# Last stage of a four-layer gated kernel: low halves of the expert weights moved to GpSimd, tile flags spread over the first tiles, and a new order of steps

## The reference, cut to what matters

```python
scores = softmax(xf @ gate_w.T)                  # 4096 tokens, 8 experts
top_vals, top_idx = top_k(scores, 2)
w_dense = zeros((T, E)).at[rows, top_idx].set(top_vals)
y, g = split(einsum('td,ehd->teh', xf, W1), 2)   # H = 192
eo = einsum('teh,edh->ted', y * silu(g), W2)
z = einsum('te,ted->td', w_dense, eo)
z = z + gated_mlp(xf, Ws1, Ws2)                  # a shared expert, 384 wide
x = x + tanh(g_ffn[1]) * z
```

## Time and profile before

| | |
|---|---|
| median of 3 runs | 1037.29 us (1036.86 to 1037.44) |
| the profiled execution's own time | 1033.01 us |
| its span | 1031.3 us |
| TensorE matmuls busy | 940.7 us, 91% |
| TensorE weight loads busy | 798.2 us, 77% |
| VectorE busy | 769.5 us, 75% |
| ScalarE busy | 575.9 us, 56% |
| GpSimd busy | 398.8 us, 39% |
| mean granted TensorE clock | 0.963 of full |

### The profile page before, as it was taken

The page is one execution under the profiler, slowest core; times in us unless marked ns, Lnnn a source line. Parts: engine busy times, 40 slices in busy tenths (PEclk is TensorE's granted clock), DMA queues, the critical chain, the costliest instruction groups (busy, mean ns, idle before and its releaser), DMA issues.

```text
span 1031.3 us, 22818 instructions
## 1 busy us (share of the span) xinstructions
PE 940.7 (91%) x6365; PEld 798.2 (77%) x6365; DVE 769.5 (75%) x2336; ACT 575.9 (56%) x1344; POOL 398.8 (39%) x571
## 2 busy tenths in 40 slices
PE   4999999999998756999999999997999995999995
PEld 3666666666665434999999999987888884999995
DVE  3677777777775325788888888889878878888884
ACT  1688888888886632344344344443555632666663
POOL 1011111111111001354445345445577651777775
PEclk9999999999999767999999999999999997999998
DMA  7664754755730250001001001100124445777775
GB/s 216 165 156 119 173 134 122 167 136 126 165 100 1 62 174 27 27 28 53 26 26 53 26 26 41 39 7 2 33 77 134 140 138 191 126 125 129 129 128 68
DMA packets 91811, 98.41 MB, mean 95 GB/s; under 512 B 14992, under 2 KB 85472, under 8 KB 91744
## 3 DMA queue, kind: packets, MB, share of 16 engines
q1 hardware_dynamic: 77504, 79.11, 29.4%
q0 software_dynamic: 13680, 17.84, 10.1%
q10 hardware_dynamic: 560, 0.66, 0.2%
HBM read 30.18 MB, written 59.01 MB: 86 GB/s over the span
## 4 chain that ended last, share of the span: by engine, by line
PE 55%; DVE 5%; issue 1%; ACT 1%; POOL 1%; DMA 1%; POOLq 0%; DVEq 0%; ACTq 0%
PE c_out L1351 3%; PE c_turned L1362 3%; PE c_cross L1351 3%; PE c_mlp L1355 3%; PE c_hidden L1355 3%; PE c_hidden L1357 3%; PE c_hidden L1356 3%; PE c_mlp L1356 3%; PE c_mlp L1357 3%; PE m_gate L2175 2%; PE m_gate L2176 2%; PE m_gate L2177 2%; PE c_scores L1351 2%; PE c_turned L1351 1%; PE m_router L2097 1%; PE m_gate L2120 1%
## 5 line engine op out<-in xcount | busy, mean ns | idle before, releaser
L1680 POOL DMA_INDIRECT out<-early_weights,aim x71 | 110.5, 1556 | 57.9 <-DMA out<-early_weights,aim 29.0
L1167 ACT ACTIVATE f_hidden<-c_hidden,f_b 128x256 f32<-128x256 f32 x128 | 53.6, 470 | 66.4 <-PE c_hidden L1357 66.4
L1355 PE MATMUL c_mlp<-f_w_hi,f_hidden_hi 128*128 128x256 f32 x256 | 80.7, 315 | 7.5 <-DVE f_hidden_lo L1285 7.5
L1655 POOL DMA_INDIRECT sorted_rows<-m_z,slot_i x64 | 70.2, 1097 | 36.7 <-DVE slot_i L1882 19.0
L1355 PE MATMUL c_hidden<-y2T_hi,f_w_hi 128*128 128x256 f32 x256 | 77.5, 303 | 0.0
L1357 PE MATMUL c_hidden<-y2T_hi,f_w_lo 128*128 128x256 f32 x256 | 72.6, 284 | 0.0
L1356 PE MATMUL c_hidden<-y2T_lo,f_w_hi 128*128 128x256 f32 x256 | 72.6, 284 | 0.0
L1357 PE MATMUL c_mlp<-f_w_hi,f_hidden_lo 128*128 128x256 f32 x256 | 72.4, 283 | 0.0
L1356 PE MATMUL c_mlp<-f_w_lo,f_hidden_hi 128*128 128x256 f32 x256 | 72.4, 283 | 0.0
L774 PE MATMUL ps_probT<-ident,prob 128*77 128x128 f32 x512 | 68.0, 276 | 3.7 <-ACT prob L505 3.2
L622 DVE TENSOR_REDUCE mx<-ps_scores 128x8 f32<-128x616 f32 x64 | 50.9, 796 | 26.4 <-PE ps_scores L708 26.3
(11 more groups left out here) (349 smaller groups left out, 3094.4 us busy)
## 6 DMA issues: line engine op xcount, KB each, us to landing
sorted_rows<-no_row SPq DMA_DIRECT2D x15, 2340.0 KB, 12.1
m_z<-sorted_rows SPq DMA_DIRECT2D x71, 130.0 KB
early_weights<-expert_chunks SPq DMA_DIRECT2D x8, 640.0 KB, 6.2
combT<-combineT_all SPq DMA_DIRECT2D x16, 256.0 KB, 2.3
slT<-slots_all SPq DMA_DIRECT2D x16, 256.0 KB, 2.5
out<-x_all SPq DMA_DIRECT2D x8, 512.0 KB
x_all<-x SPq DMA_DIRECT2D x15, 256.0 KB, 11.3
f_w_stage<-L_xattn_w SPq DMA_DIRECT2D x4, 512.0 KB, 3.6
```

Source lines behind the costliest of these rows:

```text
L1167: last = act.activation(hf[:, q % 2, j, :], psH[:, q % 2, j, :], ACT.Relu, bias=fb1[:, c_:c_ + 1])
L1355: pe.matmul(out, lh, rh, start=start, stop=False, skip_group_check=shared)
L1655: pool.indirect_dma_start(out=sorted_rows[:, :], in_=zn[:, b % 3, t, :], in_offset=None, out_offset=bass.IndirectOffsetOnAxis(ap=slot_i[:, ...
L1680: pool.indirect_dma_start(out=self.out[:, :], in_=xo[:, i % XO, :], in_offset=None, compute_op=ALU.add, out_offset=bass.IndirectOffsetOnAx ...
```

## The change

Three edits, all in `phase_d`. (1) `expert_lo` is a step of GpSimd and no longer of VectorE. (2) `tile_flags` becomes a generator: VectorE runs a piece of it behind each of the first seven tiles' steps, where it ran whole ahead of the first tile. (3) The order is new. The table stands in the same round as the last places (ROUTE), `expert_hi` one round sooner (SHARED) and at the head of ScalarE's round, `later_rstd` and `later_stats` later, `down` all in SHARED, `result` in LATE.

```diff
-        order = [(SHARED, "hidden_lo", 2), (SHARED, "table"), (ROUTE, "zf_out", 1), (AHEAD, "scatter"),
-                 (ROUTE, "hidden", 0), (ROUTE, "turn_z", 1), (ROUTE, "z_hi"), (SHARED, "ranks"),
-                 (SHARED, "hidden_hi", 0), (SHARED, "silu", 2), (SHARED, "hidden_hi", 1), (LATE, "down", 1),
-                 (AHEAD, "rows_in"), (SHARED, "up", 2), (LATE, "down", 2), (ROUTE, "weights"), (ROUTE, "logits"),
-                 (ROUTE, "hidden", 1), (ROUTE, "places"), (LATE, "expert_hi"), (AHEAD, "z_lo"),
-                 (ROUTE, "hidden_lo", 0), (ROUTE, "later_stats"), (LATE, "expert_lo"), (ROUTE, "hidden", 2),
-                 (SHARED, "result"), (SHARED, "hidden_hi", 2), (ROUTE, "up", 0), (AHEAD, "turn_z", 0),
-                 (AHEAD, "top_two"), (ROUTE, "silu", 0), (ROUTE, "up", 1), (AHEAD, "zf_out", 0), (SHARED, "down", 0),
-                 (ROUTE, "hidden_lo", 1), (ROUTE, "tanh"), (AHEAD, "later_rstd"), (ROUTE, "silu", 1), (LATE, "flags")]
+        order = [(SHARED, "later_rstd"), (SHARED, "expert_hi"), (ROUTE, "z_lo"), (ROUTE, "up", 0),
+                 (AHEAD, "turn_z", 0), (ROUTE, "up", 1), (LATE, "result"), (SHARED, "hidden_lo", 0),
+                 (SHARED, "hidden_lo", 1), (ROUTE, "zf_out", 1), (SHARED, "hidden_hi", 0), (SHARED, "down", 0),
+                 (SHARED, "hidden", 2), (SHARED, "later_stats"), (AHEAD, "turn_z", 1), (ROUTE, "ranks"),
+                 (ROUTE, "z_hi"), (ROUTE, "top_two"), (SHARED, "hidden_lo", 2), (SHARED, "hidden_hi", 1),
+                 (ROUTE, "hidden", 0), (ROUTE, "weights"), (SHARED, "down", 1), (SHARED, "silu", 2),
+                 (SHARED, "down", 2), (AHEAD, "rows_in"), (LATE, "expert_lo"), (SHARED, "hidden_hi", 2),
+                 (AHEAD, "zf_out", 0), (ROUTE, "silu", 0), (ROUTE, "hidden", 1), (ROUTE, "places"), (ROUTE, "tanh"),
+                 (ROUTE, "up", 2), (ROUTE, "table"), (ROUTE, "scatter"), (AHEAD, "logits"), (ROUTE, "silu", 1)]
...
+            def expert_lo(e):
+                pool.wait_ge(weh_done.sem, e + 1)
+                pool.tensor_tensor(el[:, e, :], self.stage_expert(e), eh[:, e, :].bitcast(F32), ALU.subtract).then_inc(wel_done.sem, 1)
...
-            unrolled(pool, order, dict(scatter=scatter, later_rstd=later_rstd), NBLK)
+            unrolled(pool, order, dict(scatter=scatter, expert_lo=expert_lo, later_rstd=later_rstd), NBLK)
...
-            def expert_lo(e):
-                dve.wait_ge(weh_done.sem, e + 1)
-                dve.tensor_tensor(el[:, e, :], self.stage_expert(e), eh[:, e, :].bitcast(F32), ALU.subtract).then_inc(wel_done.sem, 1)
...
                 dve.tensor_tensor(past_block[:], ends, spread(late_end[:].rearrange("p (e a) -> p e a", a=1), 2, NBLK), ALU.is_le)\
                    .then_inc(t_step.sem, 1)
+                yield
                 step(17)
...
+            flags_program = tile_flags()
             for i in range(XT + 1):
                 if i < XT:
                     x_hidden(i)
...
                 if i + 2 < XT:
                     x_zlo(i + 2)
                     aims(i + 2)
+                next(flags_program, None)
```

## The result

The changed kernel takes 1062.07 us (median of 4 runs, 1057.34 to 1064.04), the kernel before 1037.07 on the same chip (1033.32 to 1037.44): a ratio of 1.0264, 95% interval 1.0225 to 1.0303. On another chip the same pair gave 1.0301 (1.0254 to 1.0348). It is 25 us slower; I had forecast 18.9 and a time of 1056.2, in a range of 1040 to 1070.

A forecast was written before the change was run, and what follows sets the result against it. The last stage was bound by TensorE in eight blocks, VectorE in a gap, then expert tiles. Tile 0 14.6 us later plus 4.3 in the tail made 18.9; 1037.3 + 18.9 = 1056.2 us, range 1040 to 1070.

The forecast's parts named there:

- The stalls, 15.4 us: TensorE's waits in the last stage's token blocks, from late expert loads: 6.9 + 5.7 + 2.8 = 15.4 us.
- T(7): Start of `up(7, 0)`, block 7's matmuls on TensorE: 837.73 before, forecast at 853.1.
- the three turns: Two-block rounds through places, scatter, expert_lo, load and expert_hi: 34.2 us against TensorE's 31.4, with extras in the first two.
- The price of expert_lo, 3.2 us: On GpSimd, taken as its 128x512 `y2b` median of 1293 ns times 2.5; bounds 1.4 and 5.0 us.
- The gap, T(7) + 30.7: Last block to tile 0: places 10.2, scatter 11.1, two expert_lo 2 x 3.3, then 2.8 us; tile 0 at 883.8.
- VectorE's own line, T(7) + 25: VectorE's work from block 7 to tile 0, places through last result: ready at T(7) + 25, covered by GpSimd's queue.
- Rival 1, the shared read path: Each expert_lo holds VectorE's two-input work throughout, in three turns and the last block: 4 x 3.2 = 12.8 us more, 1069; chance 0.18.
- Rival 2, loads hidden: ScalarE's slack hides the loads, GpSimd's queue behind the last block stands: tile 0 at 868.4, time 1041; chance 0.12.
- Rival 3, faster: VectorE's gap was the only bound and GpSimd keeps up: tile 0 at 862.7, time 1035 or 1031; chance 0.16.
- the loop: Scatter delays expert_lo, then the expert load, then expert_hi and the next block's z_hi on ScalarE: 34.2 us a turn.
- The tail, 4.3 us: GpSimd's adds after tile 0: spread flags delay the first add 11.3 us, 7.0 is caught up, 4.3 stays.
- The reading of the median: The forecast increase of 18.9 us was added unchanged to the three runs' median, 1037.3, though the profiled execution took 1033.0.

The follow-up runs named there:

- the two sister kernels of the repairs together: Changed kernel with expert_hi behind rows_in and a wait ahead of the last two expert_lo: flags whole 1042.15 us (1.0076), flags spread 1048.09 us (1.0112).
- the two built from it: Kernel before with one part of the change each: only expert_lo on GpSimd, 1093.14 us (1.0527); only tile_flags spread over seven tiles, 1040.39 us (1.0018).

## Why the prediction was right, and where it wasn't

- **The direction and the range**: right. The change is slower, and by stalls in the blocks, gap and tail, of which the blocks are the largest, as in the sum.
- **The stalls, 15.4 us**: 16.4 measured, T(7) at 853.61 for 853.1. The place, the waits and the instruction were right. But the closeness is partly luck: the three turns cost 6.1, 6.2 and 4.1 for a forecast of 6.9, 5.7 and 2.8. The third turn, forecast as 10.2 + 11.1 + 3.3 + 4.7 + 4.9, was 13.3 + 10.3 + 3.0 + 4.4 + 4.6 (scatter at T(5) + 13.3, expert_lo at 841.62, load from 844.61 to 849.04, T(7) at 853.61). Scatter, expert_lo, load and the chain behind it were 1.8 us cheaper together; the scatter began 3.1 us later, 2.9 of it since `top_idx_f` at 822.55 was held across an expert_lo.
- **The price of expert_lo, 3.2 us**: 2.94. Scaling GpSimd's row of 128x512 by the columns served well, if a little high; that a fixed part is the reason is likely, but no run shows it.
- **The gap, T(7) + 30.7**: the step that failed, measured 37.4. Scatter and the two expert_lo took 1.7 us less than in the sum, the held `top_idx_f` cost 3.3 and the held last hidden_lo 5.1 (4.6 us went when it was kept apart from the pair). I had written that VectorE's own line, T(7) + 25, is covered by GpSimd's; with the hold the two are in series.
- **Rival 1, the shared read path**: its mechanism is there, in the turns and in the last block. Its total wasn't: it adds 12.8 us to the forecast, and 6.1 to 9.0 were missing. In the blocks cheaper pieces paid for it; in the gap it set the end. Counted by holds it was nearly right: of its four, with 3.2 us each, the one in the first turn cost nothing, the `hidden_lo` in the second took 3.1 us longer, `top_idx_f` in the third 2.9, and the last block had two, 3.3 and 5.1, which is 14.4 for 12.8. My own sum had these holds at nothing, and was 5.0 us too dear in the rest of the three turns and 1.7 in the gap. The Trainium skill, SBUF — State Buffer, "Who interferes with whom", has the one issued later fully blocked. The trace agrees that the hold is full; but by the records the held VectorE operation is in two cases the earlier one, by 0.48 us (857.74 and 858.22) and by 0.23 us (877.12 and 877.35), and it stays held over two GpSimd instructions. Starts on GpSimd are rough in these records, so they don't settle which was issued first.
- **Rival 2, loads hidden**: wrong; expert_hi waited 28.6 us for them in the profile, 25.6 in the rows above and 3.03 at 865.74, behind T(7). **Rival 3, faster**: wrong; even with no stall in the blocks, the time is 1% above before.
- **Whose queue**: the mechanism told was incomplete. I put the loop down to GpSimd's scatter between the places and expert_lo. The runs show the loop with and without GpSimd; what all the stalling kernels share is an expert_hi that ScalarE reaches before its load can have landed, and the changed kernel's stalls go when only that is moved.
- **The tail, 4.3 us**: 5.6. The mechanism is there, a late first add of which a part is caught up, but the size is not settled. With the flags whole, four profiles have tails of 154.4 to 154.7 us; with the flags spread, ten have 155.8 to 161.1, though the first add stands 19.8 to 20.6 us behind tile 0 in all of them. The price was 1.4 in the kernel before, 5.3 and 6.5 in two pairs of kernels with the new order. The five spread kernels whose first output comes 6.5 to 7.0 us behind tile 0 have 155.8 to 158.6, the five with 7.2 to 7.9 have 158.3 to 161.1; whether that is the cause, no run shows.
- **The reading of the median**: the span grew by 27.3, the median by 25.0. Taking the difference as it stands was right to about 2 us.

## What to carry to other kernels

When a producer step moves in a static order, follow the ring that it closes (buffer free, load, first consumer, what is queued behind that consumer) and compare the ring's length with the bound engine's time for as many blocks; an instruction that waits for a load belongs behind the work of its round that others need, not at its head. Work moved from VectorE to GpSimd is no longer in VectorE's queue, but can still hold it: look which VectorE operations fall beside it, above all in a stretch where VectorE sets the end, and put a wait there so that the two don't meet. A step that delays the first of a long chain of adds may cost more than it saves at the start, if the chain has too little slack to catch up.

## What the runs showed of the hardware

- A VectorE copy of 128x8 numbers from uint32 to fp32 took 3.48 us beside a GpSimd subtraction, and 0.17 at 787.01 of the same profile, with none beside it; a 128x512 subtraction took 6.55 us beside two of them back to back, and 0.69 when kept apart.
- GpSimd's subtraction of 128x1280 fp32 numbers took 2.88 to 2.96 us in all its 8 executions in the changed kernel (the last two as a pair of 5.76), held VectorE or not; VectorE's own takes 1.48.
- Loads of 640 KB landed 4.0 to 4.5 us after the expert_lo that released them. The median on the page of the profile is 4.4, against 6.2 before; of the 14 profiles nine have 4.4 to 4.5 and five 6.0 to 6.2. Why is open.
- Late starts with no releaser named, behind up to 5.7 us of idle time, appear in ScalarE and VectorE in seven of the 14 profiles: 10 each, at the same steps, in the two sister kernels of the repairs together, 9 in the kernel with both (expert_hi moved and expert_lo on VectorE), 4 in the kernel before and 5 in each of the two built from it, 2 in the one with rstd moved. Neither profile of the changed kernel has any, nor has either of the one with expert_hi moved alone. That kernel ran in its profiled execution 9 us faster than its median, twice. The cause stays open.
